# Moving half of the anchor fold and three weight transposes behind the first cross scores

## The reference

```python
h = _topk_cross_attn(h, context, w_q, b_q, w_kv, b_kv, w_co, b_co)
...
top_s, top_i = jax.lax.top_k(scores, TOPK)
attn = jax.nn.softmax(top_s, axis=-1)
```

```python
evidence = jnp.einsum('btp,bph->bth', weights, v)
combined = jnp.concatenate([nx, evidence, anchor], axis=-1)
h = jax.nn.silu(jnp.einsum('btc,ecr->bter', combined, e_w1) + e_b1)
expert_out = jnp.einsum('bter,erh->bteh', h, e_w2) + e_b2
return x + g * (routed @ out_w + out_b)
```

## Time and profile before

| | |
|---|---|
| median of three runs | 1450.2 us |
| profiled execution | 1446.67 us |
| its span | 1444.8 us |
| TensorE busy | 1411.6 us, 98% |
| VectorE busy | 1015.4 us, 70% |
| ScalarE busy | 840.4 us, 58% |
| mean granted TensorE clock | 0.996 |

### The profile page before, as it was taken

The page is one execution under the profiler, slowest core; times in us unless marked ns, Lnnn a source line. Parts: engine busy times, 40 slices in busy tenths (PEclk is TensorE's granted clock), DMA queues, the critical chain, the costliest instruction groups (busy, mean ns, idle before and its releaser), DMA issues.

```text
span 1444.8 us, 30134 instructions
## 1 busy us (share of the span) xinstructions
PE 1411.6 (98%) x9805; PEld 1196.0 (83%) x9805; DVE 1015.4 (70%) x4628; ACT 840.4 (58%) x2555; POOL 427.7 (30%) x613
## 2 busy tenths in 40 slices
PE   7999999999999999999999999999999999999997
PEld 5778888888888888888888788888888878887886
DVE  3586859587695868769595786959587685958642
ACT  3474475757566384756757366674857547574433
POOL 1314132233324232331334132233234313222302
PEclk9999999999999999999999999999999999999999
DMA  7620000000000000010010000000010000000000
GB/s 244 193 76 2 1 7 20 6 29 9 19 30 16 1 1 26 2 33 3 20 37 1 15 2 16 11 21 15 9 49 1 16 1 5 5 2 8 1 4 11
DMA packets 27340, 34.98 MB, mean 24 GB/s; under 512 B 3324, under 2 KB 22448, under 8 KB 26929
## 3 DMA queue, kind: packets, MB, share of 16 engines
q1 hardware_dynamic: 27185, 33.07, 7.2%
HBM read 28.83 MB, written 4.22 MB: 23 GB/s over the span
## 4 chain that ended last, share of the span: by engine, by line
PE 86%; DVE 9%; issue 2%; SPq 1%; ACT 1%; DMA 1%; POOL 0%; DVEq 0%; ACTq 0%; POOLq 0%
PE bank L955 13%; PE bank L910 13%; PE bank L979 11%; PE bank L962 7%; PE bank L919 6%; PE bank L783 6%; PE bank L769 5%; PE bank L842 4%; PE bank L894 4%; PE bank L830 4%; DVE knocked L2187 3%; PE bank L822 2%; PE bank L740 2%; PE bank L754 2%; PE bank L804 1%
## 5 line engine op out<-in xcount | busy, mean ns | idle before, releaser
L910 PE MATMUL bank<-hB,Wm 128*128 128x256 f32 x1024 | 242.3, 383 | 2.2 <-ACT hB L1356 2.2
L910 PEld LDWEIGHTS bank<-hB,Wm 128*128 128x128 f32 x1024 | 190.6, 190 | 33.3 <-issue 7.0
L955 PE MATMUL bank<-nxT,W1nx 128*128 128x256 f32 x896 | 211.5, 382 | 0.0
L1395 ACT ACTIVATE prob<-bank,rmax 128x128 f32<-128x128 f32 x512 | 180.3, 433 | 28.2 <-DVE rmax L2135 28.2
L1746 POOL TENSOR_TENSOR scores<-scores,M 128x308 f32<-128x308 f32 x128 | 94.4, 737 | 319.4 <-DVE knocked L2187 317.0
L1402 ACT ACTIVATE probT<-bank 128x512 f32<-128x512 f32 (+1 forms) x256 | 140.0, 618 | 82.2 <-PE bank L894 76.4
L979 PE MATMUL bank<-W2p,gT 128*128 128x256 f32 x768 | 183.2, 381 | 3.0 <-DVE acc L2266 1.9
L955 PEld LDWEIGHTS bank<-nxT,W1nx 128*128 128x128 f32 x896 | 165.7, 190 | 22.9 <-issue 2.8
L979 PEld LDWEIGHTS bank<-W2p,gT 128*128 128x128 f32 x768 | 141.2, 190 | 23.8 <-issue 2.8
L1434 ACT ACTIVATE tbs<-bank,b1half 128x256 f32<-128x256 f32 x128 | 60.7, 474 | 143.2 <-PE bank L910 102.3
L1450 ACT ACTIVATE tbs<-bank,betaH 128x256 f32<-128x256 f32 x224 | 95.6, 489 | 82.7 <-PE bank L962 82.7
(11 more groups left out here) (232 smaller groups left out, 2712.3 us busy)
## 6 DMA issues: line engine op xcount, KB each, us to landing
Wm_g<-in_L_xcond_w_m_dram SPq DMA_DIRECT2D x4, 1024.0 KB, 5.4
W1ev<-in_L_xcond_e_w_dram SPq DMA_DIRECT2D x6, 512.0 KB, 7.3
x<-in_x_dram SPq DMA_DIRECT2D x16, 128.0 KB, 2.3
x<-in_x_dram SPq DMA_DIRECT2D x32, 64.0 KB, 2.3
Wm<-in_L_xcond_w_m_dram SPq DMA_DIRECT2D x1, 2048.0 KB, 8.5
out_dram<-acc SPq DMA_DIRECT2D x16, 128.0 KB, 1.7
out_dram<-acc SPq DMA_DIRECT2D x32, 64.0 KB, 2.0
batch_rows<-row_store SPq DMA_DIRECT2D x4, 384.0 KB, 3.7
```

The source lines that it names most:

```text
L910: m = pe.matmul(bank_of(name)[:, half * UT:(half + 1) * UT], Wm1[:, k, c:c + P], hB[:, k, :], start=(k == 0), stop=(k == CB - 1))
L955: pe.matmul(bank_of(name)[:, n * UT:(n + 1) * UT], W1nx[:, k, c0 + n * P:c0 + (n + 1) * P], nxT[:, k, :], start=(n == 0 and k == 0), stop= ...
L1395: m = act.activation(prob[:, s, i, :], psum[s][:, i * P:(i + 1) * P], ACT.Exp, bias=rmax[:, t, s * HPS + i:s * HPS + i + 1], accum_out=rsu ...
```

## The change

In TensorE's prologue the last of the four parts of the anchor fold, both transposes of expert 1's second weights and the transpose of Wk move from ahead of the first cross scores to behind them. Eight idle products take the place of the anchor's last part, now behind a wait for the bank of `ln2`. Of the nine idle products behind the first cross scores four stay. On VectorE the reads of `anchor`, `t10` and `wk` move in among the first top-k steps, and `FOLDS_DONE` follows the new order. ScalarE, GpSimd and SyncE keep theirs.

```diff
--- before.py
+++ after.py
@@ -400,7 +400,7 @@
         ]
         FOLDS_DONE = [
             "cols", "mS", "cT", "cK", "cV", "mR", "bv", "g25", "g8", "t01", "t00", "b01",
-            "p00", "p01", "anchor", "t10", "t11", "b2", "wk", "p11", "p10", "wq", "t20", "t21",
+            "p00", "p01", "b2", "anchor", "t10", "t11", "wk", "p11", "p10", "wq", "t20", "t21",
             "MT", "r0", "p21", "p20", "r1",
         ]
         CONTEXT = {"cT": (readA, 1), "cK": (readA, 2), "cV": (values_read, 1)}
@@ -1039,22 +1039,22 @@
                 pe.wait_ge(gatedA, 2)
                 a_project("pv", oT, "so", Wso_g, 0)
                 fold_anchor(2)
-                fold_anchor(3)
+                wait_free(pe, "ln2", 0)
+                idle_in_values(8)
                 a_turn_query(0)
-                fold_turn_second(1, 0)
-                fold_turn_second(1, 1)
                 pe.wait_ge(q2_loaded, 16)
                 a_query(0)
                 fold_expert_biases("b2", (2,))
-                fold_turn("wk", wk_sb)
                 pe.wait_ge(readA, 2)
                 a_cross_scores(0, range(SLOTS), 0)
+                fold_anchor(3)
                 wait_free(pe, "pv", 1)
-                idle_in_values(2)
                 a_turn_input(1)
-                idle_in_values(5)
+                fold_turn_second(1, 0)
+                idle_in_values(4)
                 a_cross_scores(1, range(SLOTS), 0)
-                idle_in_values(2)
+                fold_turn_second(1, 1)
+                fold_turn("wk", wk_sb)
                 a_q(1)
                 a_k(1)
                 a_v(0, 1)
@@ -2336,19 +2336,19 @@
                 wait_drained(dve, "so", 0)
                 ln_stats(1, xs[0], 0)
                 ln_apply(1, xs[0], xnA, 0)
-                fold_anchor()
                 wait_full(dve, "ln2", 0)
                 ln_apply(0, xs[1], xnA, 1)
-                read_fold("t10", e2T[0], fold_psum("t10")[:, :])
                 dve.wait_ge(fold_full, FOLD_FULL["b2"])
                 expert_bias("b2", (2,))
-                read_fold("wk", wkT[:, :, :].rearrange("p h c -> p (h c)"), fold_psum("wk")[:, :])
                 halve_expert_biases()
                 a_topk("a", 0, 0, 0)
                 a_topk("a", 0, 1, 0)
+                fold_anchor()
                 a_topk("b", 0, 0, 0)
+                read_fold("t10", e2T[0], fold_psum("t10")[:, :])
                 a_topk("a", 0, 2, 0)
                 a_topk("a", 0, 3, 0)
+                read_fold("wk", wkT[:, :, :].rearrange("p h c -> p (h c)"), fold_psum("wk")[:, :])
                 a_bias_queries(1)
                 a_topk("b", 0, 1, 0)
                 a_topk("b", 0, 2, 0)
```

## The result

The change made the kernel slower by 0.14%, little more than this measurement can tell from nothing. Twenty timed runs of each: before 1451.37 us median (mean 1451.26), after 1453.2 us median (1449.95 to 1456.21, mean 1453.19). The ratio is 1.0014, with a 95% interval of 1.0007 to 1.0020, so 1.0 to 2.9 us, by the means 1.9. The forecast was 1450.9 us, in a range of 1447.6 to 1452.9. The profiled execution of the changed kernel took 1452.73 us with a span of 1450.8 us.

A forecast was written before the change was run, and what follows sets the result against it. TensorE holds 86% of the chain; in the prologue the token chain sets the pace to 67 us, then VectorE. Earlier scores -2.8, reads +2.1, stall +1.4 give +0.7 us on 1450.2: 1450.9 us, range 1447.6 to 1452.9.

The forecast's parts named there:

- Ahead of the transposed queries: TensorE's prologue up to the transposed queries: nothing moves; 0.2 us more of idle products and the new ln2 wait cost nothing.
- Start of the cross scores: First cross scores in the prologue: start near 62.9 instead of 65.69, 2.8 us earlier if the clock is full.
- VectorE's work behind D: VectorE behind its first top-k step: three reads that were free before now add 2.1 us.
- TensorE's work behind D: TensorE behind the first top-k step: t10 waits about 2 us for VectorE's read; VectorE stalls 0.3 us at full clock.
- The clock behind D: Behind the first top-k step: the fall near 60 us moves there, TensorE loses 1.1 us, VectorE's stall becomes 1.4.
- the longer fall: Half clock twice as long, through unit 1's queries and keys: up to 1.9 us more, 1453.8 us; chance 0.04.
- The sum: Whole kernel, likeliest case of one moved fall: +0.7 us on the median of 1450.2, so 1450.9; chance 0.45.
- No fall behind D: Rival: no clock fall behind the first top-k step, sum -0.4 us, 1449.8 us; chance 0.2.
- Both falls: Rival: clock drops near 60 us and again behind the first top-k step, +1.7 us, 1451.9 us; chance 0.17.
- Reads free: Rival: a later prologue wait absorbs VectorE's added reads, the whole 2.8 us is kept, 1447.4 us; chance 0.08.
- scores no earlier: Rival: something else holds the first cross scores, VectorE's 2.1 us stays alone, 1452.3 us; chance 0.04.

The follow-up runs named there:

- a1_fill: The changed kernel with eight more idle products in TensorE's wait between unit 1's input and t10; median 1450.72 us, ratio to before 0.9999.
- c1_cols: The changed kernel with all four anchor parts ahead of the output projection and eight 128-column idle products in the last part's place; ratio to before 1.0032.
- b1_extra_copies: The kernel before with three throwaway 128x512 copies on VectorE where the changed kernel has its moved reads; ratio to before 0.9999.
- a3_no_idle: The changed kernel without the eight idle products ahead of the transposed queries; traced at 8.45 us from the transposed queries to the first MAX.
- a1_fill_again: Second trace of the changed kernel with eight more idle products in TensorE's wait ahead of t10; 37.65 us from the transposed queries to the second maxima.
- c2_act_reads: The changed kernel with eight idle products in TensorE's wait and the copies of t10 and wk on ScalarE instead of VectorE; ratio to before 0.9999.
- after_again2: Third trace of the changed kernel, nothing edited; 38.45 us from the transposed queries to the second maxima.

## Why the prediction was wrong

Point by point, in the order of its steps.

Ahead of the transposed queries: right. Nothing moved there but by chance.

Start of the cross scores: right in kind, full clock at the query product, 2.5 us for the forecast 2.8 against the same trace, and 2.3 against the mean of the five traces of before, in which the first MAX came at 7.67 to 8.36. The scores came 0.35 later, counted from the transposed queries, than I had put them.

VectorE's work behind D (the first MAX): 2.1 forecast, 2.0 found (30.43 - 28.08 - 0.31 in a1_fill, the same in c1_cols). b1_extra_copies shows that such work comes out.

TensorE's work behind D: right. The wait of 1.91 us stood for some 2, and the stall at full clock, 0.31, for 0.3.

The clock behind D: this step failed, by its size. That the fall moves and does not go was right, and it was the likeliest case. But I gave it 1.1 us of TensorE's work lost, from one fall that would last from 2.5 to 5.9 us behind D, and so VectorE 1.4 us of stall. It lasted from 1.8 to 8.7, from 3.9 to 7.3 and from 1.5 to 8.3 us behind D: twice as long in two traces, and in the third as long as forecast but later, so that none of it fell into the wait. From t10 to the queries of unit 1 TensorE took 5.39, 4.71 and 5.24 us, against 3.12 at full clock in c1_cols (72.92 to 76.04): 2.3, 1.6 and 2.1 us lost, and stalls of 2.41, 1.73 and 2.26. I had named the longer fall, but only for the queries and keys and with 0.04. I had also placed the whole stall at the first pick and said that the queries' bias keeps some room. With the low clock it had none: in each trace 1.04 us of stall stood ahead of it, 0.25 to 0.93 ahead of the copy of wk, and only 0.44 ahead of the pick.

The sum: forecast -2.8 + 2.1 + 1.4 = +0.7. Found, on the means of the traces, -2.3 + 2.0 + 2.3 = +2.0 (2.09 before rounding), with 1.9 timed. The last term is what the way from the first MAX to the second maxima grew by (4.36), less the reads at full clock (2.04); 2.1 of it is shown as stalls. Two terms were off by 0.5 and 0.9 in the same direction.

The time itself missed by 2.3 us (1453.2 for 1450.9) and fell 0.3 us outside the range. Only 1.1 of that is the change. The other 1.2 is the base: the median of three runs (1450.2) lay 1.2 under that of twenty. With the right base the same sum would have given 1452.1, and a range as wide around it would have held the result, though the term for the clock would have been as wrong, 1.4 for 2.3 us. The profiled execution of before had the low clock less often than nearly all other runs, so its 3.5 us under the median were rightly called spread.

The rivals. No fall behind D: the first trace of a1_fill shows it, and with 36.32 us to the second maxima it lies 0.1 under the first trace of before, where I had put it 0.4 under. Both falls: in no trace of the changed kernel, but a3_no_idle has both; the idle products are what parts them. The Trainium skill (page "TensorE: Matmul & The Clock Gate", section "HAM oscillation — how this bites in real kernels") tells of waits between groups of matmuls that lower the clock. The waits it describes are longer than any in this stretch, so it is no rule for the falls here, and I read it too widely. What these runs add is that the clock also falls without such a wait: c1_cols waits 1.86 us and keeps it, and a1_fill_again loses it with the wait filled. Reads free and scores no earlier: both excluded by the rows of the changed kernel.

## What to carry to other kernels

Count a move on the engine that sets the pace behind it too: 2.5 us won ahead of the first top-k step bought 2.0 us of reads that had cost nothing while VectorE waited. Before work is moved behind a wait that an in-order engine must serve first, follow who waits for what stands behind it; here two chains, VectorE's steps and TensorE's road to the next unit's keys, were within 0.3 us of each other, and shortening one alone gave 0.2 us (c2_act_reads). And where a run's clock varies, cut several traces at the same marks before and after: the difference of 2 us was steady between two marks while the spans of the changed kernel's three traces lay up to 6 us apart.

## What the hardware showed that was not expected

- The clock fell while TensorE was shown busy, in the transposes right behind four-column products (after_again2, 68.8 us) and in a1_fill_again in the midst of 128-column idle products (69.6 us); with the same wait and no four-column products it stayed full twice.
- VectorE's copy of 128x512 took 0.69 us out of PSUM and 0.42 within SBUF.
- The span of one and the same kernel varied with where the clock fell: the kernel before 1446.4 to 1453.0 us over its timed runs, with granted clocks from 0.996 to 0.992.
